# Graph layers on one core: operands of the aggregations moved to PSUM, four row buffers, and placing with transposed float32 one-hots

## The chip, the cores and the metric

The kernel runs on one core of one Trainium2 chip. What counts is the device time of one execution in microseconds (us). The engines are named as in the profile: PE multiplies matrices (PEld is its loading of weights), DVE and ACT work element by element, POOL here mostly issues indirect DMAs whose descriptors it makes itself, and SP issues plain DMAs.

## What is computed

A graph of 12500 nodes with 64 values each and 200000 edges, sorted by `dst`. Two layers, each on a normalised input and added to `x`:

```
h = relu(layernorm(x))
h1 = relu(mean over the edges into a node of h[src] @ W1l.T + b1 + h @ W1r.T)
x  = x + (mean over the edges into a node of h1[src] @ W2l.T + b2 + h1 @ W2r.T)
h = relu(layernorm(x))
msg = relu(concat(h[src], h[dst], edge_attr) @ W1 + b1) @ W2 + b2     (for each edge)
x  = x + (mean of msg over the edges that leave a node, grouped by src)
```

## The kernel before

Nodes are cut into 98 windows of 128 (`W`), edges into 196 chunks (`NCH`) of 1024 (`CE`), eight tiles of 128 each (`CH = 8`). The program runs in stages, one after another: `setup`, `project` ("conv1_in"), `sum_by_dst` (agg1), `project` ("conv2_in"), `sum_by_dst` (agg2), `second_norm`, `project` ("edge_in"), `place_edges`, `sum_by_src`, `project` ("edge_out"). Inside a stage each engine runs its own loop over the chunks, and semaphores tie them together.

**Aggregations.** In `sum_by_dst` ACT writes the index list of a chunk (L590), POOL gathers its rows with eight indirect DMAs (L584, 128 rows each, `rows` has two buffers), DVE makes two one-hot matrices, one for each of two windows (L650, `iota` in PSUM against the relative `dst` in SBUF), and PE multiplies one-hots and rows (L609). DVE adds the sums to `acc` (L679) and then frees the row buffer (L694), for which ACT waits before it writes the next index list. In the same loop DVE prepares the later sorting by `src`. In the first aggregation (`Counting`) it compares `k.iota` with `src_window` (`member`, L751), reduces (L753) and counts (L758 to L761). In the second (`Ranking`) it makes `member` (L834) and reduces it with a stride (L838); PE sums the result over the partitions (`prefix`, L792); DVE makes `places` (L844), multiplies them with `member` (`chosen`, L845), and reduces (L846 to L849). The order of DVE in a chunk is: one-hots of c, `member` of c, add of c-1, sorting of c.

**Placing.** `place_edges` computes for each edge `edge_attr @ W + b_table[dst]` and scatters it, with the number of its source, to its place in the order by `src`. SP loads the attributes of a chunk (L947) and the 128 rows of `b_table` from the least `dst` of the chunk on (L951); the table holds each value in three bf16 parts. DVE subtracts the least `dst` (L1090) and makes a one-hot with edges on the partitions (L1073). PE transposes the attributes (L1004) and the one-hot (L986), ACT copies both to SBUF (L1044, L1045), PE multiplies the attributes (L1014) and the one-hot with the three parts (L992, 24 matmuls). ACT copies the place (L1058) and the rows (L1059), DVE the sources (L1108), each once the scatter of two chunks before has landed, and POOL scatters with eight indirect DMAs (L974). On PE, `turn` of chunk c+1 comes before `products` of chunk c.

**Edge_in.** `project` turns groups of seven windows on PE (L490), multiplies them (L499), and for `b_table` splits the result into three parts: ACT L519, DVE L470 and L1333, ACT L526, DVE L475; then SP stores (L546).

## Time and profile before

| | |
|---|---|
| median of 3 runs | 7313.27 us (7310.84 to 7369.94) |
| profiled execution | 7341.54 us, span 7339.8 us |
| busy, share of the span | PE 70%, PEld 67%, POOL 73%, DVE 54%, ACT 18% |
| indirect DMAs | 3 x 1568 |

A time is in us from the start of the span unless ns is said. A row of a group of instructions gives its line, engine, operation, what it writes and reads, its count, its busy time, the mean of one in ns, and after the bar the idle time of the engine ahead of it with what ended it.

### The profile page before, as it was taken

How to read it: one execution, taken by the hardware profiler on the slowest of the kernel's cores; microseconds unless marked ns; L12 is line 12 of the kernel's file. 1: busy time of each engine (PE TensorE's matmuls, PEld its weight loads, DVE VectorE, ACT ScalarE, POOL GpSimd, SP SyncE). 2: the span in 40 equal slices, each digit the busy share in tenths (PEclk: the TensorE clock that was granted, in tenths of full speed). 3: DMA queues.
4: the chain of work that ended last, by engine and by line, in shares of the span. 5: the costliest groups of instructions: out<-in, count | busy, mean ns of one | idle time of the engine just before them, and what ended most of it. 6: DMA issues, size and time to landing. Idle time of an engine off the chain costs nothing. (4 is left out here: it accounts for less than half of the span.)

```text
span 7339.8 us, 127765 instructions
## 1 busy us (share of the span) xinstructions
PE 5118.8 (70%) x36456; PEld 4895.9 (67%) x36457; DVE 3968.6 (54%) x7168; ACT 1309.2 (18%) x2487; POOL 5347.0 (73%) x5308
## 2 busy tenths in 40 slices
PE   3666666666667777777777776666666666658888
PEld 3666666666667777777777765666666666657777
DVE  4555555555555777777777764212111222139998
ACT  1000000000001000000000002222222222239997
POOL 2777777777764777777777773777777777778886
PEclk8555555555555555555555555555555555569999
DMA  2111111111111111111111111111121111123333
GB/s 52 25 25 25 25 25 25 25 25 25 25 23 33 24 24 25 25 24 24 25 24 24 25 22 52 57 57 56 55 57 56 57 57 55 56 67 107 106 106 87
DMA packets 315375, 314.47 MB, mean 43 GB/s; under 512 B 177112, under 2 KB 177370, under 8 KB 315142
## 3 DMA queue, kind: packets, MB, share of 16 engines
q0 software_dynamic: 150528, 155.24, 9.6%
q1 hardware_dynamic: 163510, 158.44, 8.1%
q8 instruction: 21, 0.34, 0.0%
q10 hardware_dynamic: 1298, 0.30, 0.0%
q14 instruction: 18, 0.15, 0.0%
HBM read 246.95 MB, written 66.68 MB: 43 GB/s over the span
## 5 line engine op out<-in xcount | busy, mean ns | idle before, releaser
L609 PE MATMUL agg_sums<-agg_rows,agg_one_hot 128*128 128x65 f32 x12544 | 2772.5, 419 | 1221.2 <-DMA agg_rows<-h_table,agg_index 679.6
L609 PEld LDWEIGHTS agg_sums<-agg_rows,agg_one_hot 128*128 128x128 f32 x12544 | 2705.6, 332 | 1299.2 <-issue 1042.7
L584 POOL DMA_INDIRECT agg_rows<-g_table,agg_index x1568 | 1613.6, 1029 | 588.3 <-issue 483.8
L974 POOL DMA_INDIRECT sorted_edges<-place_rows,place_index x1568 | 1519.2, 969 | 609.0 <-issue 486.0
L584 POOL DMA_INDIRECT agg_rows<-h_table,agg_index x1568 | 1539.6, 982 | 564.5 <-issue 505.3
L1108 DVE COPY place_rows<-src_f 128x8 f32 (+1 forms) x196 | 34.8, 177 | 1535.1 <-DMA sorted_edges<-place_rows,place_index 1534.3
L590 ACT CAST agg_index<-src_f 128x8 uint32 (+1 forms) x392 | 77.1, 197 | 4075.7 <-DVEq L694 4069.9
L679 DVE TENSOR_TENSOR acc<-acc,agg_sums 128x130 f32 x392 | 114.0, 291 | 1164.2 <-PE agg_sums L609 1164.2
L1004 PE MATMUL place_attr_ps<-ident,place_attr 128*128 128x128 f32 x784 | 212.0, 425 | 717.0 <-DVE place_hot L1073 706.2
L1014 PE MATMUL place_rows_ps<-edge_attr_w,place_attr_t 128*128 128x64 f32 x3136 | 705.2, 419 | 0.4 <-PE place_rows_ps L992 0.4
L1014 PEld LDWEIGHTS place_rows_ps<-edge_attr_w,place_attr_t 128*128 128x128 f32 x3136 | 688.6, 331 | 0.5 <-issue 0.5
L1004 PEld LDWEIGHTS place_attr_ps<-ident,place_attr 128*128 128x128 f32 x784 | 139.6, 216 | 742.5 <-issue 448.1
L650 DVE TENSOR_TENSOR agg_one_hot<-agg_iota,dst_rel 128x1024 f32<-128x1024 f32 x392 | 479.8, 1224 | 13.5
L650 DVE TENSOR_TENSOR agg_one_hot<-agg_iota,agg_shifted 128x1024 f32<-128x1024 f32 x392 | 475.5, 1213 | 0.0
L1296 POOL TENSOR_TENSOR by_src_left<-by_src_left,by_src_parts 128x512 f32<-128x512 f32 x293 | 331.1, 1130 | 86.4 <-ACT by_src_left L1280 73.5
L1242 PE MATMUL by_src_a_ps<-a_parts,by_src_hot_t 128*128 x7032 | 316.2, 194 | 76.8 <-issue 71.0
L1242 PEld LDWEIGHTS by_src_a_ps<-a_parts,by_src_hot_t 128*128 128x128 bf16 x7032 | 260.6, 98 | 147.2 <-issue 125.3
L1186 DVE TENSOR_TENSOR by_src_hot<-by_src_iota,by_src_rel 128x1024 bf16<-128x1024 f32 x293 | 353.9, 1208 | 0.1
L1300 POOL TENSOR_TENSOR by_src_parts<-by_src_left,by_src_parts 128x512 bf16<-128x512 f32 x293 | 331.7, 1132 | 0.0
L1268 ACT COPY by_src_hot_t<-by_src_hot_ps 128x1024 bf16<-128x1024 bf16 x293 | 296.5, 1012 | 65.6 <-PE by_src_hot_ps L1231 55.0
L992 PEld LDWEIGHTS place_rows_ps<-place_b_win,place_hot_t 128*128 128x128 bf16 x4704 | 299.4, 137 | 0.0
L838 DVE TENSOR_REDUCE agg_edges<-agg_member 128x98 f32<-128x784 bf16 x196 | 288.1, 1470 | 6.7
(168 smaller groups left out, 5904.8 us busy)
## 6 DMA issues: line engine op xcount, KB each, us to landing
by_src_edges<-sorted_edges SPq DMA_DIRECT2D x293, 260.0 KB, 2.6
place_attr<-in_edge_attr SPq DMA_DIRECT2D x195, 256.0 KB
agg_rows<-h_table,agg_index POOLq DMA_INDIRECT x1568, 2.4
agg_rows<-g_table,agg_index POOLq DMA_INDIRECT x1568, 2.5
sorted_edges<-place_rows,place_index POOLq DMA_INDIRECT x1568
place_b_win<-b_table SPq DMA_DIRECT2D x196, 48.0 KB
b_table<-edge_in_rows SPq DMA_DIRECT2D x14, 336.0 KB, 2.7
h_table<-conv_in_rows SPq DMA_DIRECT2D x14, 224.0 KB, 2.4
```

The lines of the kernel that those rows point to most:

```text
L584: pool.indirect_dma_start(rows[:, h, t, 0:D], None, table, bass.IndirectOffsetOnAxis(ap=index[h][:, t:t + 1], axis=0)).then_inc(landed[h], 16)
L609: mm = pe.matmul(to[:, 0:D1], hot[:, t, :], rows[:, h, t, :], start=(t == 0), stop=(t == CH - 1), skip_group_check=True)
L650: return dve.tensor_tensor(to, wide(iota[:, 0:W], 1, shape), wide(rel, 2, shape), ALU.is_equal)
L974: pool.indirect_dma_start(k.sorted, bass.IndirectOffsetOnAxis(ap=index[h][:, t:t + 1], axis=0), rows[h][:, t, :], None).then_inc(scattered ...
L992: mm = pe.matmul(rows_ps[h][:, t, :], hot_t[h][:, t, :], b[:, i * D:(i + 1) * D], start=False, stop=(t == CH - 1 and i == PARTS - 1), skip ...
L1004: pe.transpose(attr_ps[h][:, j, :], attr[h][:, j * P:(j + 1) * P], k.ident[:])
L1014: pe.matmul(rows_ps[h][:, t, :], attr_t[h][:, t // 2, :], k.edge_attr_w[:, t % 2, :], start=(t == 0), stop=False, skip_group_check=True)
L1186: dve.tensor_tensor(hot[r][:], wide(iota[:, 0:W], 1, shape), wide(rel[r % SHORT][:], 2, shape), ALU.is_equal).then_inc(hot_ready, 1)
L1242: mm = pe.matmul(a_ps[r % 2][:, t, :], hot_t[r % 2][:, t, :], k.a_parts[:, window, i, :].rearrange("p w d -> p (w d)"), start=(i == 0), st ...
L1268: act.copy(hot_t[r % 2][:], hot_ps[r % 2][:]).then_inc(hot_t_ready, 1)
L1296: pool.tensor_tensor(left[r % SHORT][:], left[r % SHORT][:], parts[r][:, :, 0, 0:D], ALU.subtract).then_inc(left_ready, 1)
L1300: pool.tensor_tensor(parts[r][:, :, 2, 0:D], left[r % SHORT][:], parts[r][:, :, 1, 0:D], ALU.subtract).then_inc(third_ready, 1)
```

## The change

Three edits and what goes with them. In the aggregations, `member` reads iota from the copy in PSUM, `places` is kept in a free part of the PSUM tile `before_ps`, and `rows`, the index lists and their semaphores come in four (`AHEAD`) rather than two; the loops run over four chunks a turn. In placing, the one-hot is made with the nodes on the partitions, as PE needs it: the chunk's ids (`dst`, int32) are copied from one row of memory to 128 partitions (`dst_row`), and DVE compares them with the number `least + partition` (`target`, in PSUM); transposes, ACT's copy and L1090 go. The one-hot and `b_table` are float32, so there is one matmul for each tile of edges instead of three, and `b_table` is stored without parts. In `setup` the least `dst` itself is kept in place of the relative one.

```diff
@@ sum_by_dst @@
-        rows, one_hot = o.tmp("rows", [P, 2, CH, D1]), o.tmp("one_hot", [P, 2, 2, CH, W])
-        index, shifted = pair(o.tmp, "index", [P, CH], U32), o.tmp("shifted", [P, CH])
+        rows, one_hot = o.tmp("rows", [P, AHEAD, CH, D1]), o.tmp("one_hot", [P, 2, 2, CH, W])
+        index, shifted = several(AHEAD, o.tmp, "index", [P, CH], U32), o.tmp("shifted", [P, CH])
...
-            with pool.Fori(0, NCH // 2) as i:
-                for h in range(2):
+            with pool.Fori(0, NCH // AHEAD) as i:
+                for h in range(AHEAD):
@@ Counting, Ranking @@
-        link(dve, dve.tensor_tensor(self.member[:], wide(self.k.iota[:, 0:WINDOWS], 2, shape),
+        link(dve, dve.tensor_tensor(self.member[:], wide(self.iota[:, 0:WINDOWS], 2, shape),
...
+        self.places = self.before_ps[:, 2, 0:WINDOWS]
...
-        dve.tensor_tensor(self.member[h][:], wide(self.k.iota[:, 0:WINDOWS], 1, shape),
+        dve.tensor_tensor(self.member[h][:], wide(self.iota[:, 0:WINDOWS], 1, shape),
...
-        link(dve, dve.tensor_tensor(self.places[:], self.before_ps[:, 0, 0:WINDOWS], k.next_place[:], ALU.add), self.step, 5 * c + 1)
-        link(dve, dve.tensor_tensor(self.chosen[:], self.member[h][:], wide(self.places[:], 1, [P, CH, WINDOWS]), ALU.mult), self.step, 5 * c + 2)
+        link(dve, dve.tensor_tensor(self.places, self.before_ps[:, 0, 0:WINDOWS], k.next_place[:], ALU.add), self.step, 5 * c + 1)
+        link(dve, dve.tensor_tensor(self.chosen[:], self.member[h][:], wide(self.places, 1, [P, CH, WINDOWS]), ALU.mult), self.step, 5 * c + 2)
@@ place_edges, SP @@
                 sp.dma_start(b_win[h][:], k.b_table[bass.ds(least, W), :]).then_inc(b_landed[h], 16)
+                if n >= 2:
+
+                    sp.wait_ge(product, c - 1)
...
+                    sp.dma_start(dst_row[h][:], dst[0:FULL * CE].rearrange("(c e) -> c e", e=CE)[bass.ds(c, 1), :].to_broadcast([W, CE])).then_inc(dst_landed[h], 16)
@@ place_edges, PE @@
                 for t in range(CH):
-                    for i in range(PARTS):
-                        mm = pe.matmul(rows_ps[h][:, t, :], hot_t[h][:, t, :], b[:, i * D:(i + 1) * D], start=False,
-                                       stop=(t == CH - 1 and i == PARTS - 1), skip_group_check=True)
+                    mm = pe.matmul(rows_ps[h][:, t, :], hot_t[h][:, t, :], b[:], start=False, stop=(t == CH - 1), skip_group_check=True)
...
-                wait_alone(pe, hot_ready, c + 1)
-                if n >= 2:
-
-                    wait_alone(pe, hot_t_ready, c - 1)
+                if n >= 2:
+
+                    wait_alone(pe, attr_ready, c - 1)
                 for j in range(CH // 2):
-                    pe.transpose(attr_ps[h][:, j, :], attr[h][:, j * P:(j + 1) * P], k.ident[:])
-                turn_hot(h, hot[h]).then_inc(turned, 1)
+                    mm = pe.transpose(attr_ps[h][:, j, :], attr[h][:, j * P:(j + 1) * P], k.ident[:])
+                mm.then_inc(turned, 1)
@@ place_edges, ACT @@
                 act.copy(attr_t[h][:], attr_ps[h][:]).then_inc(attr_ready, 1)
-                act.copy(hot_t[h][:], hot_ps[h][:]).then_inc(hot_t_ready, 1)
@@ place_edges, DVE @@
-            link(dve, dve.tensor_copy(iota[:, 0:W], k.iota[:]), iota_set, 1)
+            link(dve, dve.tensor_tensor(target[:, 0:NCH], k.least[:], k.part_no[:].to_broadcast([P, NCH]), ALU.add), target_set, 1)
...
-            def make_hot(to, offset):
-
-                return dve.tensor_tensor(to[:], wide(iota[:, 0:W], 1, shape), wide(offset[:], 2, shape), ALU.is_equal)
+            def make_hot(h, node):
+
+                return dve.tensor_tensor(hot_t[h][:], dst_row[h][:].rearrange("w (p t) -> w t p", t=CH), wide(node, 2, [W, CH, P]), ALU.is_equal)
...
-                    dve.wait_ge(turned, c - 1)
-                link(dve, dve.tensor_scalar(rel[h][:], k.dst_rel[:, bass.ds(c, 1), :].rearrange("p c t -> p (c t)"), k.least_rel[:, bass.ds(c, 1)], None, ALU.subtract),
-                     rel_ready, c + 1)
-                make_hot(hot[h], rel[h]).then_inc(hot_ready, 1)
+                    dve.wait_ge(product, c - 1)
+                dve.wait_ge(dst_landed[h], 16 * (used + 1))
+                make_hot(h, target[:, bass.ds(c, 1)]).then_inc(hot_t_ready, 1)
@@ program @@
-                project(nc, k, "edge_in", D, k.edge_ends, feed_norm, False, k.b_table, keep_own(k.edge_b1), parts=PARTS)
-            place_edges(nc, k, io["edge_attr_64"])
+                project(nc, k, "edge_in", D, k.edge_ends, feed_norm, False, k.b_table, keep_own(k.edge_b1))
+            place_edges(nc, k, io["edge_attr_64"], io["dst"])
```

## Rows read from the trace of the kernel before

**Rows 1.** The page: busy time and share; GB/s in 40 equal slices

```profile
PE 5118.8 (70%) x36456; PEld 4895.9 (67%) x36457; DVE 3968.6 (54%) x7168; ACT 1309.2 (18%) x2487; POOL 5347.0 (73%) x5308
...
GB/s 52 25 25 25 25 25 25 25 25 25 25 23 33 24 24 25 25 24 24 25 24 24 25 22 52 57 57 56 55 57 56 57 57 55 56 67 107 106 106 87
```

**Rows 2.** Groups on POOL, 165 to 2185 and 2300 to 4388 us

```profile
L584 POOL DMA_INDIRECT agg_rows<-h_table,agg_index x1551 | 1515.3, 977 | 506.2 <-issue 500.4 <-ACT agg_index L590 5.8
...
L584 POOL DMA_INDIRECT agg_rows<-g_table,agg_index x1551 | 1597.4, 1030 | 492.0 <-issue 479.2 <-ACT agg_index L590 12.8
```

**Rows 3.** Instructions by tile: ns of one (least/median/most), first and last start

```profile
L584 POOL DMA_INDIRECT agg_rows<-h_table,agg_index x1568: 946/952/7157, 135.2 to 2184.9; - x196
...
L584 POOL DMA_INDIRECT agg_rows<-g_table,agg_index x1568: 946/952/1754, 2272.7 to 4386.8; - x196
...
L974 POOL DMA_INDIRECT sorted_edges<-place_rows,place_index x1568: 963/969/1031, 4526.1 to 6541.6; - x196
```

**Rows 4.** Timeline of the second aggregation: start, length, engine, line; in brackets idle before

```profile
3006.80 0.26 DVE L844 TENSOR_TENSOR agg_places<-agg_before_ps,next_place 128x98 f32<-128x98 f32 x1 [0.51 <-PE agg_before_ps L792]
3007.09 0.98 DVE L845 TENSOR_TENSOR agg_chosen<-agg_member,agg_places 128x784 f32<-128x784 bf16 x1
3007.53 1.36 POOL L584 DMA_INDIRECT agg_rows<-g_table,agg_index  x1 [0.30 <-issue]
...
3008.88 7.06 PE L609 MATMUL agg_sums<-agg_rows,agg_one_hot 128*128 128x65 f32 x32 [2.12 <-DMA agg_rows<-g_table,agg_index]
...
3010.31 1.22 DVE L650 TENSOR_TENSOR agg_one_hot<-agg_iota,dst_rel 128x1024 f32<-128x1024 f32 x1
3010.45 0.95 POOL L584 DMA_INDIRECT agg_rows<-g_table,agg_index  x1 [0.30 <-issue]
...
3012.58 0.96 DVE L834 TENSOR_TENSOR agg_member<-iota,src_window 128x784 bf16<-128x784 f32 x1
3012.96 1.40 POOL L584 DMA_INDIRECT agg_rows<-g_table,agg_index  x1 [0.30 <-issue]
3013.58 1.47 DVE L838 TENSOR_REDUCE agg_edges<-agg_member 128x98 f32<-128x784 bf16 x1
...
3015.63 0.55 PEld L792 LDWEIGHTS agg_before_ps<-agg_edges,before 128*128 128x128 f32 x2
...
3016.89 0.26 DVE L844 TENSOR_TENSOR agg_places<-agg_before_ps,next_place 128x98 f32<-128x98 f32 x1 [0.51 <-PE agg_before_ps L792]
```

**Rows 5.** Timeline of the start of the second aggregation

```profile
2270.88 0.93 DVE L639 MEMSET agg_rows<- 128x1040 f32 x1 [2.55 <-PEq L416]
...
2297.41 0.95 POOL L584 DMA_INDIRECT agg_rows<-g_table,agg_index  x1 [4.88 <-ACT agg_index L590]
```

**Rows 6.** Timeline of the last group of `edge_in`

```profile
4507.29 0.53 ACT L519 CAST edge_in_rows<-edge_in_rows_ps 128x448 bf16<-128x448 f32 x1 [0.67 <-PE edge_in_rows_ps L499]
...
4509.64 0.62 DVE L475 TENSOR_TENSOR edge_in_rows<-edge_in_left,edge_in_rows 128x448 bf16<-128x448 f32 x1 [0.63 <-ACT edge_in_rows L526]
```

**Rows 7.** Timeline of placing

```profile
5012.95 1.09 PE L1004 MATMUL place_attr_ps<-ident,place_attr 128*128 128x128 f32 x4 [4.02 <-DVE place_hot L1073]
...
5013.83 1.06 PE L986 MATMUL place_hot_ps<-ident_b,place_hot 128*128 128x128 bf16 x8
...
5014.68 3.62 PE L1014 MATMUL place_rows_ps<-edge_attr_w,place_attr_t 128*128 128x64 f32 x16
...
5015.48 1.02 ACT L1045 COPY place_hot_t<-place_hot_ps 128x1024 bf16<-128x1024 bf16 x1
...
5018.10 1.49 PE L992 MATMUL place_rows_ps<-place_b_win,place_hot_t 128*128 128x64 bf16 x24
...
5019.71 0.97 POOL L974 DMA_INDIRECT sorted_edges<-place_rows,place_index  x1 [0.30 <-issue]
...
5020.88 0.58 ACT L1059 COPY place_rows<-place_rows_ps 128x512 f32<-128x512 f32 x1
```

**Rows 8.** DMAs by issue (KB, us to landing), and the timeline of setup

```profile
setup_rel_i<-windows SPq DMA_DIRECT2D x1, 98.0 KB, 2.9
...
38.05 1.23 DVE L376 CAST acc<-setup_dst_ids 98x2048 f32<-98x2048 int32 x1 [34.68 <-DMA setup_dst_ids<-in_dst]
```

More of the change, by code:

```diff
@@ L48 @@
 SHORT = RING // 2
+AHEAD = 4
 ACT_T = 5
@@ L387, in _ @@
             dve.tensor_scalar(count[:], count[:], 1, None, ALU.add)
-            dve.tensor_scalar(span[:], span[:], 1, None, ALU.add)
-            dve.tensor_tensor(rel[:], least_f[:], first_f[:], ALU.subtract).then_inc(windows_made, 1)
+            dve.tensor_scalar(span[:], span[:], 1, None, ALU.add).then_inc(windows_made, 1)
             for a in range(2):
@@ L590, in put_index @@
                 act.copy(index[h][:], k.src[:, bass.ds(c, 1), :].rearrange("p c t -> p (c t)")).then_inc(index_ready[h], 1)
-            for h in range(2):
+            for h in range(AHEAD):
                 put_index(h, h)
-            with act.Fori(1, NCH // 2) as i:
-                for h in range(2):
+            with act.Fori(1, NCH // AHEAD) as i:
+                for h in range(AHEAD):
                     act.wait_ge(rows_used[h], i)
-                    put_index(2 * i + h, h)
+                    put_index(AHEAD * i + h, h)
         @block.tensor
@@ L604, in _, with add_up, chunk @@
             pe.reg_mov(windows, 0)
-            def add_up(to, hot, h):
+            def add_up(to, hot, q):
                 for t in range(CH):
-                    mm = pe.matmul(to[:, 0:D1], hot[:, t, :], rows[:, h, t, :], start=(t == 0), stop=(t == CH - 1), skip_group_check=True)
+                    mm = pe.matmul(to[:, 0:D1], hot[:, t, :], rows[:, q, t, :], start=(t == 0), stop=(t == CH - 1), skip_group_check=True)
                 return mm
-            def chunk(c, h, used, first):
+            def chunk(c, q, used, first):
+                h = q % 2
                 count = pe.value_load(k.win_row[0:1, bass.ds(NCH + c, 1)], min_val=1, max_val=WINDOWS)
                 s.prefix(pe, c, h)
-                wait_alone(pe, landed[h], 16 * CH * (used + 1))
+                wait_alone(pe, landed[q], 16 * CH * (used + 1))
                 pe.wait_ge(hot_ready, c + 1)
@@ L628, in chunk @@
                         pe.wait_ge(more_ready, pe.snap(windows, min_val=1, max_val=NCH * WINDOWS))
-                        add_up(more_sums, more_hot, h).then_inc(more_product, 1)
-            for h in range(2):
-                chunk(h, h, 0, True)
-            with pe.Fori(1, NCH // 2) as i:
-                for h in range(2):
-                    chunk(2 * i + h, h, i, False)
+                        add_up(more_sums, more_hot, q).then_inc(more_product, 1)
+            for q in range(AHEAD):
+                chunk(q, q, 0, q < 2)
+            with pe.Fori(1, NCH // AHEAD) as i:
+                for q in range(AHEAD):
+                    chunk(AHEAD * i + q, q, i, False)
         @block.vector
@@ L706, in _ @@
             s.sort(dve, 0, 0)
-            both(1, 1)
-            with dve.Fori(1, NCH // 2) as i:
-                both(2 * i, 0)
-                both(2 * i + 1, 1)
-            add(NCH - 1, 1, *windows_of(NCH - 1))
+            for q in range(1, AHEAD):
+                both(q, q)
+            with dve.Fori(1, NCH // AHEAD) as i:
+                for q in range(AHEAD):
+                    both(AHEAD * i + q, q)
+            add(NCH - 1, AHEAD - 1, *windows_of(NCH - 1))
             dve.wait_ge(added, NCH)
@@ L1100, in window @@
                     dve.wait_ge(more_done, number)
[L1101 to L1102 removed]
+                    link(dve, dve.tensor_tensor(shifted[:], target[:, bass.ds(c, 1)], k.window_neg[:, bass.ds(w, 1)], ALU.subtract), more_shifted, number)
+                    make_hot(h, shifted[:]).then_inc(more_hot, 1)
                 further_windows(dve, c, window)
```

99 lines of the change are left out of this document (47 added, 52 removed).

## The prediction, made before the changed kernel ran

> **What bounds the kernel now.** I read the engines' busy shares first: POOL is the busiest at 73%, yet none is full [rows 1], so the bound must be looked for by stage. Three stages hold most of the span: the two aggregations (`sum_by_dst`) and the placing (`place_edges`). In each POOL issues 196 x 8 = 1568 indirect DMAs, the first and last at 135.2 and 2184.9, 2272.7 and 4386.8, 4526.1 and 6541.6 us [rows 3]. So they take 2050, 2114 and 2015 us, 6179 of 7340.
>
> The second view is the same instruction grouped by stage. In placing a DMA takes 969 ns in the median [rows 3], and its pace of 2015.5/1567 = 1286 ns leaves 317 ns between two. In the second aggregation the time between two is the same, 492.0/1551 = 317 ns, but the mean is 1030 ns against a median of 952; in the first the mean is 977, and 506.2/1551 = 326 ns lie between [rows 2, 3]. So POOL sets the pace of all three, placing runs at its floor already, and the aggregations lie above it, in the length of some DMAs and a little in waits.
>
> The third view, the timeline, says which DMAs are long. The one at 3007.53 takes 1.36 us: `chosen` (L845) had started at 3007.09 and ends at 3008.07. The one at 3012.96 takes 1.40 while `member` (L834) runs from 3012.58 to 3013.54. Each ends 0.82 us after the end of the DVE operation. The DMA at 3010.45, under a one-hot (L650), keeps 0.95 [rows 4]. L834 and L845 (L751 in the first aggregation) read both operands from SBUF; the one-hot reads iota from PSUM, and the reductions have one operand. I read this as a lock: an indirect DMA that begins inside such an operation waits for its end.
>
> The Trainium skill, "SBUF — State Buffer", section "Who interferes with whom", says that a DVE instruction with two SBUF inputs contends with a GpSimd instruction that reads SBUF, and one with a single SBUF input does not. The same section reports a probe in which tensor_tensor did not stall a DMA of GpSimd at all; by that sentence the edit would free nothing, and it stands below as rival 1. The trace is with the first sentence: the stretched DMAs of [rows 4].
>
> **The change, part by part.**
>
> Aggregations, operands. L751, L834 take iota from PSUM, L845 the places from PSUM; each keeps one SBUF operand. Price of the lock, mean less median: first aggregation 1551 x (977 - 952) ns = 39 us, second 1551 x (1030 - 952) ns = 121 us [rows 2, 3]. I let all of it go: -160. What remains with two SBUF operands (L758, L759, L760, L849, at most 0.26 us long) is kept in the median. The start of the first aggregation, with a DMA of 7157 ns under L1307 [rows 3], lies outside the counted stretch and stays. Are the operations longer with PSUM? The one-hot with a PSUM operand takes 1.22 us for 1024 elements, `member` with none 0.96 for 784 [rows 4]: both are 1.05 ns an element and 0.14 over. So I add nothing; doubling what is over would add 0.3 us a chunk to DVE, to be set against its slack.
>
> That slack: in the second aggregation DVE runs from L844 (3006.80) to the end of L838 (3015.05), 8.25 us, and the next prefix on PE, from 3015.63 to L844 at 3016.89, needs 1.26 [rows 4]: a loop of 9.5 us. POOL's floor is 8 x (0.952 + 0.317) = 10.15. PE's own work is 7.06 + 1.3 = 8.4. So POOL stays last, by 0.6 us.
>
> Four row buffers. They take away what POOL waits for an index list: 506.2 - 492.0 = 14 us in the first aggregation, of which I take 10 because part of it may be time of issue rather than waits, and the wait of 4.88 before 2297.41 in the second [rows 2, 5]: -15. POOL can run three chunks further ahead, which buys nothing more, as it never catches up with itself. The memset of `rows` (L639), ahead of POOL's first DMA, doubles from 0.93 us [rows 5]: +0.9 each time, +2.
>
> `edge_in` without three parts. Of the last group's work the store can follow the copy (ends 4507.82) instead of L475 (ends 4510.26) [rows 6]: -2.5. Before that DVE and ACT are released by PE, group for group, and I take nothing.
>
> Placing, on PE. Removed per chunk: 8 transposes (1.06 us) and 24 bf16 matmuls (1.49). Added: 8 float32 matmuls of the shape of L1014, which take 3.62. With 1.09 for the transposes of attr PE goes from 7.26 to 1.09 + 3.62 + 3.62 = 8.3 us of a chunk of 8 x 1.286 = 10.29 [rows 7]: hidden under POOL. ACT loses the copy of 1.02 us. On DVE L1090 goes, and the one-hot stays one operation of 1024 elements, 1.22 us, now with an int32 operand read with a stride. The nearest strided row is L838, 1.47 us for 784 [rows 4], which by size bounds it at 1.9 us. DVE's work in placing is this one-hot and small operations, so 8 us of a chunk are idle. It has one SBUF operand, so no lock.
>
> Placing, on the queues. SP issues one more DMA a chunk, 128 partitions x 4 KB = 512 KB, behind the one for b_win and behind a wait for product(c-2). Queued behind it is attr of the next chunk. Then: product(c-2), transfer, one-hot, the second half of product(c). PE needs some 16.6 us for two chunks and POOL 20.4; the chain is 0.5 + transfer + 1.9 + 3.6, so the transfer may take 14 us. Nearest row: 98 KB copied from one row to 128 partitions, landed 2.9 us after the issue [rows 8]. By size (5.2 times) that is 15.1 if none of the 2.9 is fixed, and 9 if half is; below, 2.9 itself. I take 4, as a copy of 4 KB pieces should cost less a byte than one of 784 byte pieces. It adds 50 GB/s to 56; by-source lives with 107 [rows 1]. Scatters that land later are covered: ACT fills the rows by 5021.46, and POOL, whose chunk began at 5019.71, wants them at 5029.9 [rows 7]. Steady placing: 0.
>
> Start of placing. The first one-hot now waits for attr, b_win and the ids (256 + 32 + 512 KB), attr of chunk 1 comes behind them, and PE turns that before product 0: with 4 us for the copy, less the transposes and ACT's copy that go, plus 2.1 of matmul I get +4, between +1 and +8.
>
> Sum: -160 - 15 + 2 - 2.5 + 4 = -171. The profiled execution took 7341.5 us (span 7339.8), so 7170 for one like it, a span of 7168. The median of the three runs is 7313.3, 28 lower, with one run at 7369.9. If these differences lie in by-source or elsewhere, the median falls to 7142; if they are the lock's own (how often a DMA begins inside an operation is a matter of phase), they go with it and it falls to 7170. I can't tell, and take 7157.
>
> **Rivals.**
> 1. The operands are not the cause, and only the buffers act. Against it: every kind of DVE operation overlaps DMAs, and only those with two SBUF operands stretch them. -15 + 3.5: 7301. Chance 0.05.
> 2. DVE and PE take over in the second aggregation. If the three operations cost 0.3 us each more with PSUM, the loop is 10.4: 196 x 0.25 = 49 us are given back, and 7206 results. Chance 0.07.
> 3. Placing gets slower, by the copied ids. In setup DVE waited 34.68 us, to 38.05, for the ids, 776 KB: 22 GB/s [rows 8]. If the copy of one row runs like that, 512 KB take 24 us, placing 196 x 24 = 4.7 ms, the kernel 9.8 ms. It cancels the gain at 171/196 = 0.87 us a chunk more, that is from 11.0 us per 512 KB on. Against it: the 98 KB copy. Chance 0.04. The Trainium skill, "DMA: Bandwidth & Descriptors", section "Why a DMA increments its semaphore by 16 and not by 1", says that the number of engines is the largest up to 16 that divides the slowest dimension; the slow load has 97 partitions, so one engine, and the new copy has 128, so 16. The trace agrees on the slow one; none of its rows shows 512 KB.
> 4. Something smaller in placing (a strided one-hot that still takes the lock). Two operations of 0.96 to 0.98 us cost 121/196 = 0.62 us a chunk, 0.32 per us; 1.2 to 1.9 us then cost 77 to 118 us: 7234 to 7275. Chance 0.05.
>
> **Numbers.** The forecast has 0.79. Its own range runs from 7142 less 17 (7 for the rest of the waits and a start of placing at +1, 10 for a chain of `edge_in` that gains as well) to 7170 plus 20 (once the phases are fixed, a DMA could begin under a small operation in each chunk, 196 x 0.1): 7125 to 7190, 7157 taken. The range for 8 in 10 adds half of what rival 2 costs above and a little below: 7120 to 7205. A difference under 1%, 73 us, can't be told from none here. Faster by over 1% (below 7240): the forecast, rival 2 and half of 4: 0.88. Within 1%: rival 1 and the other half of 4: 0.08. Slower: rival 3: 0.04.
>
> **What would show it.** Aggregations: POOL's mean at 952 to 955 ns in both, idle 317 ns, first to last DMA about 1995 us each; no DMA above 1 us but at the start. L834, L845 at 0.96 to 1.0 us. If the mean stays near 1030, the lock was read wrongly (rival 1); if it falls and POOL waits for an index list, it is rival 2. Placing: 2015 us from first to last, DMAs at 969 ns, PE 8.3 us a chunk; longer DMAs under the new one-hot mean rival 4, POOL waiting for `place_rows` means rival 3. The forecast is wrong most easily in placing, where four things change and only POOL's pace hides them.

## The result, and the profile after

| | before | changed |
|---|---|---|
| median | 7325.74 us (7310.84 to 7369.94, 4 runs) | 7132.94 us (7107.34 to 7161.97, 4 runs) |
| profiled execution, its span | 7341.5, 7339.8 us | 7132.94, 7131.2 us |
| ratio | | 0.973, 95% interval 0.967 to 0.979 |

Predicted were 7157 us with a range of 7120 to 7205. The median lies inside it, 24 us below the value.

The first view is the page of the changed kernel, busy time and GB/s in 40 slices, which answers [rows 1]:

```profile
PE 5414.0 (76%) x33320; PEld 5138.6 (72%) x33321; DVE 4039.5 (57%) x6943; ACT 1103.0 (15%) x2276; POOL 5182.2 (73%) x5309
...
GB/s 52 26 26 26 26 26 26 26 26 26 26 25 38 26 26 26 26 26 26 26 26 26 26 36 112 104 106 106 104 104 107 105 104 104 105 85 107 107 106 71
```

POOL is busy 165 us less. PE is busy 295 us more, and placing moves 104 to 107 GB/s instead of 56. The second view is the indirect DMAs by stage, to be held against [rows 2, 3]: first the groups (mean ns before the bar), then the tiles (least/median/most ns, first and last start).

```profile
L991 POOL DMA_INDIRECT sorted_edges<-place_rows,place_index x1568 | 1518.2, 968 | 619.0 <-issue 471.2 <-ACT place_rows L1057 128.8 <-DVE place_rows L1103 17.7
L586 POOL DMA_INDIRECT agg_rows<-h_table,agg_index x1568 | 1498.2, 955 | 532.1 <-issue 477.5 <-DVE agg_iota L643 54.6
L586 POOL DMA_INDIRECT agg_rows<-g_table,agg_index x1568 | 1491.0, 951 | 538.5 <-issue 477.5 <-DVE agg_iota L643 61.0
```

```profile
L586 POOL DMA_INDIRECT agg_rows<-h_table,agg_index x1568: 947/952/7149, 138.7 to 2113.4; - x196
...
L586 POOL DMA_INDIRECT agg_rows<-g_table,agg_index x1568: 946/952/968, 2175.3 to 4142.9; - x196
...
L991 POOL DMA_INDIRECT sorted_edges<-place_rows,place_index x1568: 963/969/1031, 4284.3 to 6306.4; - x196
```

In the second aggregation the longest DMA now takes 968 ns, where it took 1754. The mean fell from 1030 to 951. The idle time left is 477.5 us of issue for 1567 gaps, 305 ns each, and no wait for an index list. From first to last DMA, and between the stages, the profiled execution moved like this (us):

| stretch | before | changed | difference |
|---|---|---|---|
| start, to the first DMA | 135.2 | 138.7 | +3.5 |
| first aggregation | 2049.7 | 1974.7 | -75.0 |
| between (`conv2_in`) | 87.8 | 61.9 | -25.9 |
| second aggregation | 2114.1 | 1967.6 | -146.5 |
| between (`second_norm`, `edge_in`) | 139.2 | 141.4 | +2.2 |
| placing | 2015.5 | 2022.0 | +6.5 |
| rest (`sum_by_src`, `edge_out`) | 798.2 | 824.8 | +26.6 |
| span | 7339.8 | 7131.2 | -208.6 |

**The lock, in the timeline.** The same stretch of the second aggregation as [rows 4]:

```profile
3007.52 0.29 DVE L683 TENSOR_TENSOR acc<-acc,agg_sums 128x130 f32 x1 [1.22 <-PE agg_sums L611]
...
3008.62 0.97 DVE L854 TENSOR_TENSOR agg_chosen<-agg_member,agg_before_ps 128x784 f32<-128x784 bf16 x1
3009.08 0.95 POOL L586 DMA_INDIRECT agg_rows<-g_table,agg_index  x1 [0.30 <-issue]
...
3013.74 0.96 DVE L843 TENSOR_TENSOR agg_member<-agg_iota,src_window 128x784 bf16<-128x784 f32 x1
3014.11 0.95 POOL L586 DMA_INDIRECT agg_rows<-g_table,agg_index  x1 [0.30 <-issue]
```

A DMA begins 0.46 us into `chosen`, another 0.37 us into `member`, and both take 0.95. In [rows 4] a DMA 0.44 us into `chosen` took 1.36, and one 0.38 us into `member` 1.40. The operations kept their length (0.97 and 0.96, before 0.98 and 0.96): reading one operand from PSUM cost DVE nothing.

**What had not been forecast: pauses.** In every stage of the kernel before there are 13 gaps of about 2 us. They lie behind the DMAs number 113, 225, 337 and so on to 1457, always 112 apart, and the profile puts them under "issue". Two rows of the timeline of the kernel before, the 113th DMA of the first aggregation and the next:

```profile
287.14 0.95 POOL L584 DMA_INDIRECT agg_rows<-h_table,agg_index  x1 [0.30 <-issue]
290.11 1.55 POOL L584 DMA_INDIRECT agg_rows<-h_table,agg_index  x1 [2.02 <-issue]
```

Beyond the usual 0.30 us, the 13 pauses come to 24.3 us in the first aggregation, 19.2 in the second and 19.6 in placing. In the changed kernel the aggregations have none: no gap there is longer than 0.32 us. Placing still has its 13, and they got longer, 27.2 us together.

**Placing.** A timeline of the changed kernel, to be held against [rows 7], with one of the pauses in its first row:

```profile
5009.76 0.97 POOL L991 DMA_INDIRECT sorted_edges<-place_rows,place_index  x1 [2.56 <-issue]
...
5012.83 3.62 PE L1003 MATMUL place_rows_ps<-place_b_win,place_hot_t 128*128 128x64 f32 x16
...
5016.96 1.09 PE L1013 MATMUL place_attr_ps<-ident,place_attr 128*128 128x128 f32 x4 [0.50 <-PE place_rows_ps L1003]
...
5021.69 0.58 ACT L1057 COPY place_rows<-place_rows_ps 128x512 f32<-128x512 f32 x1
...
5022.22 2.03 DVE L1069 TENSOR_TENSOR place_hot_t<-place_dst_row,place_target 128x1024 f32<-128x1024 int32 x1 [0.43 <-issue]
```

And the issue of the copied ids (KB, us to landing):

```profile
place_dst_row<-in_dst SPq DMA_DIRECT2D x195, 512.0 KB, 4.1
```

PE spends 1.09 us on the transposes and 3.62 on the one-hot's products. The ids land 4.1 us after their issue, and the one-hot takes 2.03. The rows that ACT fills at 5021.69 are wanted by POOL at 5028.84. Over all chunks this slack is 8.45 us in the median, and 8.44 in the kernel before.

**Where the short stretches come from.** Tiles of the stage `conv2_in` before and changed, then of `edge_out` in the same order (least/median/most ns of one matmul):

```profile
L499 PE MATMUL conv_in_rows_ps<-conv_w,conv_in_h_t x196: 417/417/579, 2201.8 to 2266.7; 64*128 64x128 f32 x196
```

```profile
L501 PE MATMUL conv_in_rows_ps<-conv_w,conv_in_h_t x196: 271/272/579, 2130.6 to 2168.3; 64*128 64x128 f32 x196
```

```profile
L499 PE MATMUL edge_out_rows_ps<-edge_out,edge_out_h_t x196: 222/275/350, 7303.5 to 7334.9; 65*128 65x64 f32 x196
```

```profile
L501 PE MATMUL edge_out_rows_ps<-edge_out,edge_out_h_t x196: 311/421/421, 7068.3 to 7126.5; 65*128 65x64 f32 x196
```

The code of these stages is the same. The same matmul takes 417 ns in one execution and 272 in another. Between the two aggregations the granted clock was 0.50 (1.2 GHz) before and 0.83 on average in the changed kernel, where it stood at 1.00 (2.4 GHz) from 2131.6, 1 us after the first of these matmuls, to 2172.5. In the last 79 us of the kernel before it was 0.92, in the last 71 us of the changed one 0.50. The two differences, -25.9 and +26.6, are therefore no part of the change and happen to cancel.

### The profile page after: what moved, and what is told of

Same layout as the page of the kernel before. It is cut to its first block and busy times, and to the rows that moved or that the text cites. A ratio compares the mean times of both kernels' runs of the same rounds, so it can differ in the third digit from the quotient of the medians.

```text
span 7131.2 us, 119237 instructions
## 1 busy us (share of the span) xinstructions
PE 5414.0 (76%) x33320; PEld 5138.6 (72%) x33321; DVE 4039.5 (57%) x6943; ACT 1103.0 (15%) x2276; POOL 5182.2 (73%) x5309
## 5 line engine op out<-in xcount | busy, mean ns | idle before, releaser
L586 POOL DMA_INDIRECT agg_rows<-h_table,agg_index x1568 | 1498.2, 955 | 532.1 <-issue 477.5
L586 POOL DMA_INDIRECT agg_rows<-g_table,agg_index x1568 | 1491.0, 951 | 538.5 <-issue 477.5
L1003 PE MATMUL place_rows_ps<-place_b_win,place_hot_t 128*128 128x64 f32 x3136 | 709.7, 421 | 0.0
L1003 PEld LDWEIGHTS place_rows_ps<-place_b_win,place_hot_t 128*128 128x128 f32 x3136 | 692.5, 333 | 0.0
L1069 DVE TENSOR_TENSOR place_hot_t<-place_dst_row,place_target 128x1024 f32<-128x1024 int32 x196 | 395.9, 2020 | 81.9 <-issue 40.0
L1056 ACT CAST place_index<-place 128x8 uint32 (+1 forms) x196 | 38.7, 197 | 1779.4 <-DMA sorted_edges<-place_rows,place_index 1747.4
```

The lines of the kernel that those rows point to most:

```text
L586: pool.indirect_dma_start(rows[:, h, t, 0:D], None, table, bass.IndirectOffsetOnAxis(ap=index[h][:, t:t + 1], axis=0)).then_inc(landed[h], 16)
L1003: mm = pe.matmul(rows_ps[h][:, t, :], hot_t[h][:, t, :], b[:], start=False, stop=(t == CH - 1), skip_group_check=True)
L1069: return dve.tensor_tensor(hot_t[h][:], dst_row[h][:].rearrange("w (p t) -> w t p", t=CH), wide(node, 2, [W, CH, P]), ALU.is_equal)
```

## The experiments

Each ratio is against runs of the kernel before on the same chip, and spans are from the first to the last indirect DMA. The first four kernels ran on a chip where the kernel before takes 8568 us (8537.81 to 8650.73, 19 runs), 17% more than on the chip of the prediction. The other eight ran on one like that of the prediction (7362.61 and 7344.07 us).

### On the slower chip: the parts alone

Edits: `e1_operands` has the operands in PSUM and two buffers. `e2_buffers` has four buffers and loops of four chunks, with the operands in SBUF. `e3_pool_loop` changes POOL's loop alone. `e4_agg_only` has both edits of the aggregations and the old placing.

```diff
# e1_operands, against the kernel before
-wide(self.k.iota[:, 0:WINDOWS], 1, shape)
+wide(self.iota[:, 0:WINDOWS], 1, shape)
-self.places = o.tmp("places", [P, WINDOWS])
+self.places = self.before_ps[:, 2, 0:WINDOWS]
# e3_pool_loop, against the kernel before
-            with pool.Fori(0, NCH // 2) as i:
-                for h in range(2):
-                    wait_alone(pool, index_ready[h], i + 1)
+            with pool.Fori(0, NCH // turn) as i:
+                for q in range(turn):
+                    h = q % 2
+                    wait_alone(pool, index_ready[h], turn // 2 * i + q // 2 + 1)
```

> The kernel before with only the operands moved: member reads iota from PSUM, places lie in PSUM. Two row buffers, placing as before. Lock theory: POOL's DMAs fall to a mean of 952 to 955 ns in both aggregations (from 977 and 1030), which is 39 + 121 = 160 us less in all: first to last DMA 2011 and 1993 us; the waits for an index list stay or grow a little, since a faster POOL reaches the end of its two buffers sooner. The 13 pauses of about 2 us a stage stay in all three stages. Rival (the operands are not the cause): means stay at 977 and 1030, no change of time. Clock of PE in conv2_in and edge_out can move the whole by some 25 us either way, so the stages are what counts.

> The kernel before with only the four row buffers and loops of four chunks a turn in the aggregations; operands in SBUF, placing as before. Theory: the waits go (15 us), and so do the 13 pauses a stage of 2.2 and 1.8 us, 44 us in both aggregations; the lock stays, 40 us and 121 us or somewhat more or less, as the phases shift: first to last DMA 2015 and 2090 us, about 60 us less in all. Rival 1 (the pauses have to do with the operands): they stay, and only 15 us go. Rival 2 (four buffers are what freed the long DMAs): means fall to 955.

> The kernel before; only POOL's own loops are written with four chunks a turn (32 indirect DMAs in the body instead of 16) in the first aggregation and in placing; the second aggregation keeps two. Two row buffers and all else as before. Theory (the pauses hang on the length of POOL's loop): none in the first aggregation and in placing (24 and 20 us less), 13 in the second. Rival 1 (they hang on the number of row buffers or their semaphores): 13 in each stage, no change. Rival 2 (on the number of DMAs issued since the start): the same in each stage.

> The changed aggregations with the placing, the table in three parts and the set-up of the kernel before. Theory: the gain is all in the aggregations: first to last DMA 1975 and 1968 us, placing 2015 us, so about 5 to 10 us faster than the changed kernel stage for stage (placing 2022 there) and a ratio to before of 0.970 to 0.975. Rival (the new placing brings something of its own, in its start or for the stages behind it): placing and the stage behind it longer than with the new one.

| kernel | median us | ratio (95%) | first, second aggregation |
|---|---|---|---|
| e1_operands | 8533.95 | 0.996 (0.993 to 0.999) | 2402, 2394 |
| e2_buffers | 8471.55 | 0.989 (0.983 to 0.995) | 2340, 2353 |
| e3_pool_loop | 8595.02 (one run) | | 2400, 2406 |
| e4_agg_only | 8533.92 | 0.996 (0.993 to 0.999) | 2360, 2388 |

None of the four came out as expected in time, though the lock's part did. `e3_pool_loop` keeps its 13 pauses in each stage, as the first rival of its expectation said. The groups of `e1_operands`:

```profile
L584 POOL DMA_INDIRECT agg_rows<-h_table,agg_index x1568 | 1503.6, 959 | 952.6 <-issue 473.3 <-ACT agg_index L590 426.1 <-DVE agg_iota L640 53.2
L584 POOL DMA_INDIRECT agg_rows<-g_table,agg_index x1568 | 1496.3, 954 | 958.1 <-issue 469.4 <-ACT agg_index L590 428.9 <-DVE agg_iota L640 59.9
```

The means are 959 and 954 ns, so the lock is gone here too, but POOL waits 426 and 429 us for index lists. Its timeline shows who is late:

```profile
2999.59 6.61 PE L609 MATMUL agg_sums<-agg_rows,agg_one_hot 128*128 128x65 f32 x30
...
3010.56 0.29 DVE L679 TENSOR_TENSOR acc<-acc,agg_sums 128x130 f32 x1 [6.38 <-remote]
...
3011.00 0.20 ACT L590 CAST agg_index<-src_f 128x8 uint32 x1 [16.60 <-DVEq L694]
...
3011.97 0.95 POOL L584 DMA_INDIRECT agg_rows<-g_table,agg_index  x1 [4.33 <-ACT agg_index L590]
```

The products end at 3006.20 and DVE adds them at 3010.56, 4.4 us later, with DVE idle for 6.38. Over the 196 chunks of this aggregation the add begins 3.1 us after the products in the median. In `e9_operands`, which is the same kernel on a chip like that of the prediction, it begins 0.15 us after them. POOL's DMAs and the matmuls take nearly the same time on both chips (median 955 and 952 ns; 7.06 us for 32 matmuls), and DVE is busy 3939 us in the one and 3956 in the other, so it is not these that are slower. No instruction that the profile counts as busy fills the 4.4 us. The code has there reads of `win_row` into registers and branches on them, which aren't counted; that it is these, no run shows. On this chip the forecast would have failed by the mechanism of rival 2: DVE and PE's loop is the bound. Why `e2_buffers` gains more than `e4_agg_only`, which has the same buffers without the lock, is open.

The slow chip answers nothing on how the gain is shared on the chip of the prediction, so the same edits were run again there.

### The parts alone, on a chip like that of the prediction

`e7_buffers` is `e2_buffers` again and `e9_operands` is `e1_operands` again. `e6_place_only` is the changed kernel with the old aggregations. `e5_changed` is the changed kernel.

> The changed kernel itself, once more, beside the three below. If this chip is like the one of the prediction (before at about 7.3 ms): ratio 0.973, first to last indirect DMA 1975, 1968 and 2022 us in the first aggregation, the second, and placing. If it is like the one of the first four experiments (before at about 8.57 ms), where the loops of PE and DVE bound every stage: the aggregations gain what the kernel with the changed aggregations alone gained, 0.4% (about 2360 and 2388 us); for placing the theory that its time there is PE's last matmul to the message that the product is done, 6 us a chunk, says no change (2598 us), the rival that ACT's second copy and the 32 transposes and matmuls were part of the chain says a gain of about 1 us a chunk, 200 us.

> Only the placing part of the change (with edge_in and setup), the aggregations as before. My theory: the whole gain comes from the aggregations, placing gives nothing or costs a little because the scatters land later: +7 us in placing, -2.5 in edge_in, so ratio 1.000 to 1.003 on a chip like that of the prediction. Rival: the copied ids slow POOL's DMAs down enough to be measured (over 20 us, ratio over 1.003), covered in the changed kernel by the aggregations. Placing's pauses at every 112th DMA stay, and are longer (2.5 us rather than 1.8).

> Only the four row buffers and the loops of four chunks, operands in SBUF as before. On a chip like that of the prediction, theory: this takes away what POOL waits for index lists and the pauses of 2 us at every 112th DMA (24 and 24 us), and leaves the lock: 2050 - 35 = 2015 us in the first aggregation, 2114 - 24 = 2090 in the second, ratio 0.992. Rival: the pauses belong to the lock (an operation of DVE with two SBUF operands), then they stay here: 2039 and 2109 us, ratio 0.998. On a chip like that of the first experiments it repeats 0.989.

> Only the operands in PSUM, two buffers as before: the edit of the first experiment again. On a chip like that of the prediction, theory: the lock's 48 and 121 us go (long DMAs), and nothing else: first to last DMA about 2005 to 2010 us in the first aggregation and 1993 in the second; the pauses at every 112th DMA stay; ratio 0.977. With the 0.990 of the buffers alone this makes the whole, so the two parts add. Rival: the two edits overlap (with two buffers POOL, once faster, waits for index lists as it did on the slow chip), then the aggregations gain less than 35 and 110 us and POOL has idle time put down to ACT's index list.

| kernel | median us | ratio (95%) | first aggregation | second | placing |
|---|---|---|---|---|---|
| before (profile) | | | 2049.7 | 2114.1 | 2015.5 |
| e5_changed | 7148.71 | 0.973 (0.966 to 0.980) | 1975.1 | 1967.8 | 2024.7 |
| e6_place_only | 7372.35 | 1.0035 (0.9997 to 1.0072) | 2047.9 | 2112.8 | 2022.0 |
| e7_buffers | 7246.53 | 0.990 (0.982 to 0.997) | 2013.5 | 2080.8 | 2014.8 |
| e9_operands | 7203.94 | 0.9785 (0.973 to 0.984) | 2014.4 | 1997.8 | 2014.6 |

The tiles of `e7_buffers`, then of `e9_operands`:

```profile
L585 POOL DMA_INDIRECT agg_rows<-h_table,agg_index x1568: 947/952/7141, 135.5 to 2149.0; - x196
...
L585 POOL DMA_INDIRECT agg_rows<-g_table,agg_index x1568: 947/952/1746, 2210.3 to 4291.1; - x196
```

```profile
L584 POOL DMA_INDIRECT agg_rows<-h_table,agg_index x1568: 946/952/7147, 164.5 to 2178.9; - x196
...
L584 POOL DMA_INDIRECT agg_rows<-g_table,agg_index x1568: 946/952/968, 2238.8 to 4236.6; - x196
```

With the buffers alone, DMAs of up to 1746 ns stay and all pauses are gone. With the operands alone, no DMA of the second aggregation exceeds 968 ns and all 13 pauses stay (25.2 and 24.6 us beyond the usual gap). The parts add: the buffers take 36.2 and 33.3 us off the two aggregations, the operands 35.3 and 116.3, together 71.5 and 149.6, and the changed kernel has 75.0 and 146.5. So the rivals of both expectations (the pauses belong to the lock; the two edits overlap) fall.

The placing part alone costs 6.5 us in placing, 7.3 of it in pauses (26.9 us against 19.6). The ratio to before is 1.0035, with an interval that just takes in 1. The rival of its expectation wanted over 20 us in placing and falls.

### What removes the pauses

`e10_pool_loop` is `e3_pool_loop` again. `e8_four_placing` is the changed kernel with four index lists, row buffers and semaphores in placing too, and with the bias that is added to `x` at the start of the first aggregation copied to PSUM first.

```diff
# e8_four_placing, against the changed kernel
-        ... rows = ... pair(o.tmp, "rows", [P, CH, D1])
+        ... rows = ... several(AHEAD, o.tmp, "rows", [P, CH, D1])
-                if n >= 2:
-                    act.wait_ge(scattered[h], 16 * CH * used)
+                if n >= AHEAD:
+                    act.wait_ge(scattered[q], 16 * CH * at[1])
-    dve.tensor_tensor(k.x[:], k.x[:], wide(k.conv_b[1][:], 1, [P, WINDOWS, D]), ALU.add)
+    dve.tensor_tensor(k.x[:], k.x[:], wide(iota[:, W:W + D], 1, [P, WINDOWS, D]), ALU.add)
```

> Only POOL's loop over four chunks a turn instead of two, in the first aggregation and in placing; in the second aggregation it keeps two; buffers and all other engines as before. It asks what takes away the pauses of 2 us at every 112th DMA. Theory: the length of POOL's loop; then they go in the first aggregation (24 us) and placing (20 us), and stay in the second. Rival: the number of buffers and semaphores; then all three stages keep 13 pauses, as they did on the slow chip.

> The changed kernel, with four index and row buffers and a loop of four chunks in placing too (POOL, ACT, DVE), and with the bias that is added to x at the start of the first aggregation read from PSUM. Theory: as in the aggregations, the 13 pauses go: placing from 2022 to 1995 us; the stretched DMA at the start of the first aggregation (7.15 us) goes, 6 us; together 33 us off the changed kernel, ratio 0.968. Rival: the pauses come from POOL's transfers that are not yet done and not from the loop; then they stay, 6 us off. On a slower chip, where PE's loop sets the pace of placing, nothing but the 6 us changes.

`e10_pool_loop` took 7316.68 us in one run, with 2049.5, 2114.6 and 2015.2 us in the three stages, the same as before. All 39 pauses are there, in the stages with four chunks a turn as well. Two of them in its timeline, one in the first aggregation and one in placing:

```profile
289.56 0.96 POOL L585 DMA_INDIRECT agg_rows<-h_table,agg_index  x1 [2.25 <-issue]
```

```profile
4647.20 0.96 POOL L975 DMA_INDIRECT sorted_edges<-place_rows,place_index  x1 [1.80 <-issue]
```

`e8_four_placing` took 7106.63 us (7092.10 to 7123.74), ratio 0.968 (0.961 to 0.974). Its tiles:

```profile
L586 POOL DMA_INDIRECT agg_rows<-h_table,agg_index x1568: 947/952/2005, 168.4 to 2137.9; - x196
...
L996 POOL DMA_INDIRECT sorted_edges<-place_rows,place_index x1568: 965/969/1031, 4305.3 to 6301.5; - x196
```

Placing takes 1996.2 us, 28.5 less than in `e5_changed`, and has no pause; expected were 27. The longest DMA of the first aggregation is 2.0 us instead of 7.1, and that stage is 5.6 us shorter: with the bias read from PSUM, none of the DMAs that begin under the 6.69 us operation exceeds 0.95 us. What is left there is shown by its timeline:

```profile
181.10 0.91 DVE L748 CAST agg_window_i<-src_f 128x1568 int32<-128x1568 f32 x1
181.14 2.00 POOL L586 DMA_INDIRECT agg_rows<-h_table,agg_index  x1 [0.30 <-issue]
...
183.06 0.98 DVE L750 CAST src_window<-agg_window_i 128x1568 f32<-128x1568 int32 x1
183.45 1.41 POOL L586 DMA_INDIRECT agg_rows<-h_table,agg_index  x1 [0.30 <-issue]
```

Both casts have one operand, in SBUF, and yet the DMAs that begin under them are stretched. So two SBUF operands aren't the only form that does it. These casts take 0.6 ns an element, where the reductions and comparisons take 1.1 to 1.9; whether that is what sets them apart, no run shows.

The length of POOL's loop is thus not the cause; on this chip four buffers with their semaphores, or the loops of the other engines over them, are what helps. These two weren't separated. On the slower chip the same step didn't suffice: with four buffers `e2_buffers` still has 12 and 7 pauses in its two aggregations (0.5 to 1.9 us), and `e4_agg_only` has none in its first and 16 in its second, 1.87 us each and now 96 DMAs apart instead of 112. One of them:

```profile
2906.59 0.95 POOL L585 DMA_INDIRECT agg_rows<-g_table,agg_index  x1 [1.87 <-issue]
```

So the number of buffers changes where the pauses fall, and on one chip makes them vanish, but it isn't the whole cause. That POOL waits in the pause for its own transfers fits (in placing the pauses grew from 1.8 us to between 1.8 and 2.7 when the DMA engines got more to do), but no run shows what it waits for.

By its rows `e8_four_placing` is 34 us (28.5 + 5.6) better than the changed kernel. The intervals of the two ratios overlap, so the medians alone don't prove it.

### Is placing near an edge, and is it really the two operands?

`e11_ids_twice` is the changed kernel with each chunk's ids copied twice; the second copy goes to a tile that nothing reads. `e12_hot_in_sbuf` is the changed kernel with iota read from SBUF in the one-hots.

```diff
# e11_ids_twice
+                    sp.dma_start(once_more[h][:], dst[0:FULL * CE].rearrange("(c e) -> c e", e=CE)[bass.ds(c, 1), :].to_broadcast([W, CE])).then_inc(dst_landed[h], 16)
-                dve.wait_ge(dst_landed[h], 16 * (used + 1))
+                dve.wait_ge(dst_landed[h], 32 * (used + 1))
# e12_hot_in_sbuf
-                return dve.tensor_tensor(to, wide(iota[:, 0:W], 1, shape), wide(rel, 2, shape), ALU.is_equal)
+                return dve.tensor_tensor(to, wide(k.iota[:, 0:W], 1, shape), wide(rel, 2, shape), ALU.is_equal)
```

> The changed kernel with each chunk's ids copied twice (the second copy into a tile that nothing reads; DVE waits for both). It asks how much slack placing has left. By the last traces ACT refills the rows under 1 us before POOL wants them, since the scatters land late beside the copied ids. Theory A (the slack is used up by the load on the DMA engines, and 512 KB more pushes the scatters' landing past POOL's need): POOL waits for place_rows in most chunks, placing gets longer by 0.5 to 4 us a chunk, 100 to 800 us, ratio over 0.985. Theory B (the scatter is only late where it lies behind the copy, and ACT's finish is close by chance of the order): placing stays within 20 us of 2024, ratio 0.973 to 0.977.

> The changed kernel with one operand moved the other way: the one-hots of the aggregations (two operations of 1.22 us a chunk) read iota from SBUF, so that they have two SBUF operands. Theory (an indirect DMA that begins inside a DVE operation with two SBUF operands ends only when that operation does): DMAs that begin under a one-hot last as long as from their start to its end plus 0.12 us, up to 2.1 us; each aggregation gets 150 to 275 us longer than 1975 and 1968, the mean of a DMA rises to 1.05 to 1.13 us, and this form, the longest of all, costs more than member and chosen did together. Rival: the stretch belongs to the 784-element forms with a bf16 or strided operand and not to two SBUF operands: then nothing changes (within 10 us).

`e11_ids_twice`: 7133.29 us, ratio 0.9695 (0.964 to 0.975), placing 2022.5 us. Its issues and its tile:

```profile
place_dst_row<-in_dst SPq DMA_DIRECT2D x195, 512.0 KB, 4.1
place_once_more<-in_dst SPq DMA_DIRECT2D x195, 512.0 KB, 5.8
```

```profile
L993 POOL DMA_INDIRECT sorted_edges<-place_rows,place_index x1568: 963/969/1032, 4285.6 to 6308.1; - x196
```

Twice the ids cost placing nothing, so theory A falls. Its premise was a misreading of mine: I had taken the DMA at 5022.48, the fourth of a chunk, for the first of the next one, and so a slack of 6.6 us at this place for one of 0.2. Counting the DMAs of the stage by eights puts it right: it is the DMA at 5028.84 that needs the rows filled by 5022.27. With the ids twice the median slack is still 8.41 us.

`e12_hot_in_sbuf`: 7338.01 us in one run, the whole gain gone. The aggregations take 2082.2 and 2066.1 us, 107 and 98 more than in the changed kernel. Its timeline and tile:

```profile
3000.89 1.23 DVE L653 TENSOR_TENSOR agg_one_hot<-iota,dst_rel 128x1024 f32<-128x1024 f32 x1
3001.17 1.76 POOL L586 DMA_INDIRECT agg_rows<-g_table,agg_index  x1 [0.30 <-issue]
3002.03 1.22 DVE L653 TENSOR_TENSOR agg_one_hot<-iota,agg_shifted 128x1024 f32<-128x1024 f32 x1
...
3003.24 0.95 POOL L586 DMA_INDIRECT agg_rows<-g_table,agg_index  x1 [0.30 <-issue]
```

```profile
L586 POOL DMA_INDIRECT agg_rows<-g_table,agg_index x1568: 946/952/1982, 2282.2 to 4348.3; - x196
```

The mechanism is shown from the other side: the one-hot, under which no DMA was stretched in the kernel before ([rows 4]), stretches them as soon as its second operand comes from SBUF too, and by the same rule. The 191 long DMAs of the second aggregation end 0.82 us after the end of the operation that they began in, as the 290 of the kernel before did. The Trainium skill, "SBUF — State Buffer", section "Who interferes with whom", has the rule that a DVE instruction with two SBUF inputs contends with GpSimd's reads, and a probe in which tensor_tensor did not stall a DMA; by that rule the trace agrees, the probe's result isn't seen here.

The size was wrong: 107 and 98 us, where 150 to 275 stood. Of two one-hots that follow each other only one is paid for. The stretched DMA ends at 3002.93, and the next begins at 3003.24, where the second one-hot is nearly over (3003.25). The price hangs on where the next DMA falls, not on the sum of the operations' lengths: 2.44 us of locking operations cost 0.50 us a chunk (98.3/196), and `member` and `chosen`, 1.94 us but apart, cost 0.62.

## Why the prediction was right, point by point

**The bound, and the lock: right.** -160 was forecast, 39 and 121. The DMAs over 1 us lost 41 us of length in the first aggregation and 122 in the second, and `e9_operands` and `e12_hot_in_sbuf` tie this to the operands. The wording, that a DMA which begins inside such an operation waits for its end, is a little too wide: in the second aggregation of the kernel before 313 DMAs begin inside `member` or `chosen`, and 23 of them keep their 0.95 us. Of these, 3 begin in the first 0.04 us of the operation. The other 20 begin in its last 0.12, where an end 0.82 us after the operation is no later than the usual one. Nothing was added on DVE, as said (0.97 and 0.96 us).

**Four buffers: the term was mis-sized.** -15 was forecast, as POOL's waits for index lists. These went: in the first aggregation gaps of 0.33 to 0.9 us, 9.7 us beyond the usual, for which 10 stood, and in the second the one wait of 4.88 (4.6 beyond the usual), for which 5 stood. But the buffers also took 43.5 us of pauses. The step that failed is the reading of "317 ns between two" as the floor of issue. It is a mean over gaps of 305 ns and 13 long ones: 305 + 19600/1567 ns = 317 ns. So "POOL's floor is 8 x (0.952 + 0.317)", and the "about 1995 us" for each aggregation, were 20 to 27 us too high. The two stages gained 221.5 us where 175 stood. `e7_buffers` has the term by itself: 69.5 us, 57 of them waits and pauses and 12 shorter DMAs, since fewer of them were stretched (87 and 278 over 1 us, before 110 and 290).

**Small steps.** The first DMA came 3.5 us later, of which the steps had 1, for the memset; the rest of it has no explanation here. For the end of `edge_in` and the start of placing the steps gave -2.5 and +4, so +1.5. Profiles with PE at the slow pace in this stretch show +2.2 (139.2 and 141.4 us), those at the fast pace -3.5 (114.9 in `e10_pool_loop`, 111.4 in `e6_place_only`). So the +4 is too high in at least one of them, and the two terms weren't separated.

**Placing: right in the main, +6.5 for 0.** The transfer was taken at 4 us and took 4.1. The one-hot, bounded at 1.9, took 2.02 in the mean: the bound by size was too low, without effect. PE's 8.3 us stayed under POOL's 10.3. "Scatters that land later are covered" holds, with 8.45 us of slack. What was missed is again the pauses, which grew by 7.6 us beside the copied ids. `e6_place_only` shows the same 6.5, and `e8_four_placing` gets it back and more.

**The sum.** Profile to profile -171 was forecast and -208.6 measured. The difference of 38 is 46 more from the aggregations, 6.5 lost in placing, and small change. From there to the median the forecast offered 7142 or 7170 and took 7157, not knowing where the 28 us between the profiled execution and the median came from. `conv1_in`, `conv2_in`, `edge_in` and `edge_out` show it. Each takes one of two values, 25 to 29 us apart in the mean, by the pace of PE in it (272 or 417 ns for the matmul of `conv2_in`, 275 or 421 for that of `edge_out`). In the ten profiles from chips like that of the prediction, the start takes 135 to 139 us or 165 to 168, the stretch of `conv2_in` 60 to 62 or 88 to 89, the one between second aggregation and placing 110 to 115 or 139 to 143, and the rest 798 to 799 or 818 to 825. So the runs of a kernel stand on steps of some 27 us, as 7107.34, 7132.94, 7132.95 and 7161.97 do. The second of the two guesses, that the differences are the lock's own, is wrong; the first, that they lie "in by-source or elsewhere", is right.

That the forecast came within 24 us of the median is in part luck. From 7313.3 to 7157 is a change of 156 us; from median to median 193 were measured. Of the 37 missing, 12 don't show, since the median before of four runs lies 12 us above that of the three that the forecast started from. Two slips in its working changed nothing: a chunk of placing would cancel the gain from 10.29 + 0.87 = 11.2 us on, not 11.0, and 7190 plus half of 49 is 7215, not 7205.

**The rivals.** Rival 1 fell by `e9_operands`, in which the buffers stay two. Rivals 3 and 4 fell by the changed kernel's own placing, and rival 3 with a wide margin by `e11_ids_twice`. Rival 2 didn't occur here, but it decides on the slower chip, where the gain of the aggregations' part is 0.4%. A chance of 0.07 was right for the chip of the prediction and said nothing of another.

## What to carry to other kernels

Where GpSimd issues indirect DMAs all the time, the other engines' operations should be looked through for those under which DMAs are longer than elsewhere: here those with two operands in SBUF, and a few casts with one. Moving one of the two operands to PSUM cost DVE nothing here, and paid at every such DMA. A mean gap is to be taken apart before it is called a floor: list the gaps by length, and look whether the long ones come at a fixed distance. And before a slack is read off a timeline, count which item of the chunk one is looking at.

## What the runs showed of the hardware

- An indirect DMA that begins inside a DVE operation with two SBUF operands, but after its first 0.04 us, ends 0.82 us after that operation, where it wouldn't end later anyway. That was so for 290 DMAs of the kernel before in its second aggregation, and for 191 of `e12_hot_in_sbuf`, whatever the operation (0.96 to 1.23 us, f32 or bf16). At the start of the first aggregation, one under a single 6.69 us operation takes 7.15; with the bias in PSUM (`e8_four_placing`) none does.
- Two casts with one SBUF operand, of 1568 elements a partition, stretch DMAs to 2.00 and 1.41 us as well (`e8_four_placing`). The prediction gave the rule of the Trainium skill, "SBUF — State Buffer", section "Who interferes with whom", as if no instruction with a single SBUF input contended. The section leaves the 2-port perf modes out of that rule; whether these casts run in one, no run shows.
- With two buffers POOL pauses 1.7 to 2.9 us at every 112th indirect DMA, in three stages with different work. With four it doesn't on a chip like that of the prediction; on the slower chip it does in three of four aggregations, in one of them at every 96th. The cause is open.
- The granted clock in the records doesn't always tell PE's pace. In `e8_four_placing` it stands at 1.00 (2.4 GHz) from the start to beyond 3000 us, yet in `conv1_in` the matmul takes what it takes at 0.50 elsewhere:

```profile
96.00:161.00 65.00, 65.00 (x281) 55.10 (x280) 14.03 (x24) 18.77 (x26) 0.00 (x0) 1.00 0.20 46
```

```profile
L501 PE MATMUL conv_in_rows_ps<-conv_w,conv_in_h_t x196: 417/417/579, 96.2 to 161.1; 64*128 64x128 f32 x196
```

  The first row is a stretch of the windows view (stretch, its length, busy time of PE, PEld, DVE, ACT, POOL, then granted clock, DMA share, GB/s). PE is busy all of its 65 us; in the changed kernel's profile the same 196 matmuls lie between 96.2 and 131.5 us, at 272 ns. The Trainium skill, "TensorE: Matmul & The Clock Gate", section "Seeing it yourself", warns that the records of the clock have been seen to be unreliable; this case agrees.
- Two chips differ by 17% on the same kernel, in the time between operations and not in the operations: DVE's add follows the products after 3.1 us in the median on one and after 0.15 on the other.
